# Regrouping the weight slices and the chunks of a scan-and-FFN kernel on eight cores

## The chip, the cores and the metric

The kernel runs on all 8 NeuronCores of one Trainium2 chip. Each core computes one of the 8 batch rows; nothing is exchanged between cores. The metric is the device time of the slowest core, in microseconds (us).

## The reference

The input x is 8 x 2048 x 1024 in f32. Per batch row, with D = 1024, 16 states per channel and an inner size of 4096:

```python
# part 1: a selective scan
u = layernorm(x)
delta = softplus(u @ Wd.T + bd)
a_pos = softplus(a_log) + 1e-4                      # [1024, 16]
for t in range(2048):
    state = exp(-delta[t, :, None] * a_pos) * state + delta[t, :, None] * b_param * u[t, :, None]
    y[t] = state.sum(-1)
x = x + layernorm(y @ Wo.T + bo)
# part 2: a feed-forward part with quantized weights and rows
def weight_quant(w): s = 1 / clip(mean(abs(w)), 1e-5); return clip(round(w * s), -1, 1) / s
def act_quant(v):    s = 127 / clip(max(abs(v), -1), 1e-5); return clip(round(v * s), -128, 127) / s
def bitlinear(v, w): return act_quant(v) @ weight_quant(w).T
v = layernorm(x)
x = x + layernorm(bitlinear(silu(bitlinear(v, w_gate)) * bitlinear(v, w_up), w_down))
```

w_gate and w_up are 4096 x 1024, w_down is 1024 x 4096.

## The kernel before

A row of 2048 tokens is 16 tiles of 128 tokens (NC = 16). The tiles are grouped into five chunks, CHUNK = (4, 4, 4, 2, 2), and a chunk's scan runs channel by channel and state by state over all its tokens: 128 scans (8 channel blocks x 16 states) of 512 or 256 columns for each chunk, 640 in all (NSCAN). Chunk q continues from the states that chunk q - 1 left.

Part 1 of a chunk, by engine:

- SyncE (SP) loads x tiles into two buffers; VectorE takes their statistics (`stats`, bn_stats on two halves, bn_aggr, then the negated mean and the variance plus EPS as two one-column steps); GpSimd raises the latter to the power -1/2 (`rstd`) and normalizes; TensorE transposes the tile, ScalarE copies it into `s_uT`.
- Delta: TensorE multiplies with Wd (`s_w`, shared by Wd and Wo and reloaded in turn by GpSimd's queue), ScalarE makes the softplus in four activations, GpSimd adds the two halves and then makes delta * u.
- Scan k: ScalarE makes exp(-delta * a) into one of two PSUM banks (L554), GpSimd makes delta * u * b into the ring `s_dun` (L860), VectorE runs the recurrence (L694), TensorE adds up the 16 states (L383), GpSimd copies the last column of four scans into `s_state` (L869), and ScalarE moves the sum out.
- Output: Wo on TensorE, two norms, the row quantization (`quant1`), a transpose into one of five buffers `s_q1T`.

Part 2 of a tile tc: TensorE multiplies with gate and up in two groups (`gate_up(tc, 0)` and `gate_up(tc, 1)`, each 4 banks of gate and 4 of up, 8 matmuls a bank; five PSUM banks in turn), ScalarE makes silu (L615), VectorE the product (L768) into one of three buffers `s_h` of 2048 columns, then the maximum (L772), the scale, and the quantized products (L787). `down(tc)` transposes them on TensorE (L456), ScalarE copies back (L623), and 64 matmuls with w_down follow (L472), whose quantized form comes back from HBM (`tdq`) for each tile. A tile's `down` stands on TensorE between the two groups of the next tile. The last norm is added to the output by an accumulating DMA.

The quantized weights are made inside the kernel. Each of gate, up and down is cut into 32 slices of 128 x 1024, loaded through five staging buffers `stg` (NSTG = 5). A slice is loaded twice. The first pass (P1) sums its absolute values, even slices on ScalarE (L590), odd ones on VectorE (L741); TensorE then makes the mean over partitions. The second pass (P2) scales and rounds on GpSimd (L899), and ScalarE writes the signs in FP8 (L601) into `s_tg` and `s_tu`, or into `s_tq`, from where SP stores them to `tdq`. PSEQ is the order of all 192 loads; before, it is P1 of gate, up and down, then P2 of gate and up by halves, then P2 of down. `gate_up` of tile 0 waits for 32 signed slices for its first group and 64 for its second; `loads_td` waits for all 96.

Every engine executes one order written out by hand as a string. A letter is the next step of a lane, a number repeats it. On all engines `s` is a scan step (on TensorE, four scans), `a` the first norm, `b` Delta, `c` and `d` the output and its norms; `p` is a weight slice, `g` a step of part 2 (on TensorE one bank, one transpose or 8 down matmuls; on VectorE one product, a maximum, or the scales), `t` a copied transpose, `f` the last norm, `v` a state copy, `w` a load of Wd or Wo. On SP `x` loads a tile, `p` a slice, `q` stores signs, `r` loads a down block, `o` stores the first sum.

Of the kernel before, what the change touches and what calls it, by code (L numbers as in the profile page):

```python
# [7 lines left out]
F32 = mybir.dt.float32  # L8
# [20 lines left out]
CHUNK = (4, 4, 4, 2, 2)  # L29
# [85 lines left out]
def on_act(i):  # L115
    return i % 2 == 0


P1A = [sum(on_act(j) for j in range(i)) for i in range(97)]
# [4 lines left out]
def place(k):  # L124
    q, i = k // 128, k % 128
    if LEN[q] > 256:
        return k % 3, 0, k - 2
    i += 128 * (q - min(j for j in range(NQ) if LEN[j] <= 256))
    return k % 3, 256 * (i // 3 % 2), (k - i - 2 + i % 3 if i < 6 else k - 5)


def build_nc():
# [23 lines left out]
    with ExitStack() as es:  # L156
# [18 lines left out]
        s_h = SB("s_h", [128, 3, 2048], BF16)  # L175
        s_q1T = SB("s_q1T", [128, 5, KC, 128], BF16)
# [5 lines left out]
        s_dun = SB("s_dun", [128, 3, 512], F32)  # L182
# [14 lines left out]
        s_nm = SB("s_nm", [128, 4, 2, 2], F32)  # L197
# [3 lines left out]
        s_r1u = SB("s_r1u", [128, NC], F32)  # L201
        s_r2d = SB("s_r2d", [128, NC], F32)
# [31 lines left out]

        d_cst, d_bor, d_bo2, d_o = SEM("d_cst"), SEM("d_bor"), SEM("d_bo2"), SEM("d_o")
# [20 lines left out]
        def gid(tc, grp):  # L258
            return (2 * tc + grp) % 3
# [84 lines left out]
        def _(h):  # L344
# [43 lines left out]
            def out_proj():  # L388
                for tc in range(NC):
# [5 lines left out]
                    if tc == 0:  # L395
                        h.wait_ge(d_bo2, 16)
# [583 lines left out]
```

## Time and profile before

| | |
|---|---|
| time, median of 3 runs | 1418.84 us (1415.46 to 1420.03) |
| the profiled execution: its time | 1418.27 us |
| its span on the slowest core (core 0) | 1416.7 us |
| spans of the eight cores | 1403.5 to 1416.7 us |
| TensorE, VectorE, ScalarE, GpSimd busy | 1025, 1043, 898, 771 us |
| HBM read, written | 218.38 MB, 20.97 MB |

The span runs from the first to the last instruction of the core; the device time lies 1.6 us above it. Busy times are of one core. A TensorE clock of 1.00 is full speed.

### The profile page before, as it was taken

The page shows a single profiled execution, that of the slowest core. Times are in us where ns is not written, and L with a number is a line of the kernel's source. Part 1 is how long each engine was busy: PE and PEld are TensorE (multiplying, and loading weights), DVE is VectorE, ACT ScalarE, POOL GpSimd, SP SyncE. Part 2 cuts the span into 40 slices and gives each one's busy share as a digit, 9 for nine tenths or more (in the row PEclk, how much of TensorE's full clock was granted, in tenths as well). Part 3 has the DMA queues.
Part 4 walks back from the last instruction along what each step waited for, and adds up shares of the span by engine and source line. Part 5 has one row for each costly group of instructions (what it writes and reads, how often), then busy time and mean ns, then how long its engine had stood idle before and what let it go on. Part 6 is the DMA issues. An engine that isn't in the chain of part 4 may idle for free.

```text
span 1416.7 us, 21053 instructions; the slowest of 8 cores (1403.5 to 1416.7 us)
## 1 busy us (share of the span) xinstructions
PE 1025.1 (72%) x5094; PEld 473.7 (33%) x5094; DVE 1042.7 (74%) x1390; ACT 898.1 (63%) x1348; POOL 771.1 (54%) x1116
## 2 busy tenths in 40 slices
PE   0445333231766588989899879899899989989994
PEld 0211000010322144444444434444444444444442
DVE  2468999555768898789999898888677887854221
ACT  0788777787869758855567864656775576533121
POOL 1476654899878765666445566464465643430000
PEclk9967555556878699999999999999999999999997
DMA  8996988799797683525624162474137341422442
GB/s 178 281 279 209 248 269 266 246 281 266 229 276 216 210 187 102 108 50 176 152 87 135 30 157 52 125 174 135 30 120 153 101 131 27 127 93 74 132 134 75
DMA packets 69387, 223.94 MB, mean 158 GB/s; under 512 B 7441, under 2 KB 11921, under 8 KB 69266
## 3 DMA queue, kind: packets, MB, share of 16 engines
q1 hardware_dynamic: 58642, 197.43, 44.8%
q0 software_dynamic: 10624, 25.17, 11.7%
q8 instruction: 43, 0.70, 0.2%
q14 instruction: 78, 0.64, 0.2%
HBM read 218.38 MB, written 20.97 MB: 169 GB/s over the span
## 4 chain that ended last, share of the span: by engine, by line
DVE 27%; PE 26%; issue 16%; POOL 11%; ACT 10%; DMA 8%; DVEq 1%; SPq 1%; POOLq 0%; ACTq 0%
DVE s_s L694 19%; PE p_gu L437 15%; POOL s_dun L860 8%; PE p_dn L472 5%; DMA stg<-wus 3%; ACT p_ab L554 2%; POOL stg L899 2%; DVE s_qs L772 2%; DMA stg<-wgs 1%; DMA s_onesf<-onesf 1%; PE p_y L383 1%; DMA s_td<-tdq 1%; PE p_wo L402 1%; ACT s_sg L615 1%; DVE s_h L768 1%
## 5 line engine op out<-in xcount | busy, mean ns | idle before, releaser
L554 ACT ACTIVATE p_ab<-s_dl,s_nega 128x512 f32<-128x512 bf16 (+1 forms) x640 | 380.2, 601 | 266.2 <-DVE s_s L694 264.3
L694 DVE TENSOR_TENSOR_SCAN s_s<-p_ab,s_state,s_dun 128x512 bf16<-128x512 f32 (+1 forms) x512 | 489.8, 1002 | 73.5 <-POOL s_dun L860 33.7
L860 POOL TENSOR_SCALAR s_dun<-s_uT,s_bprm 128x512 f32<-128x512 bf16 (+1 forms) x640 | 386.1, 608 | 257.1 <-DVE s_s L694 255.2
L383 PE MATMUL p_y<-s_s,s_ident 128*128 128x512 bf16 (+1 forms) x640 | 169.3, 395 | 215.5 <-DVE s_s L694 212.9
L437 PE MATMUL p_gu<-s_tu,s_q1T 128*128 128x512 fp8e4 x1024 | 240.1, 387 | 29.9 <-ACT s_sg L615 19.6
L472 PE MATMUL p_dn<-s_td,s_h 128*128 128x512 fp8e4 x1024 | 235.8, 382 | 6.1 <-ACT s_t L573 3.0
L437 PE MATMUL p_gu<-s_tg,s_q1T 128*128 128x512 fp8e4 x1024 | 231.2, 380 | 4.7 <-ACT s_tu L601 2.9
L694 DVE TENSOR_TENSOR_SCAN s_s<-p_ab,s_dun 128x512 bf16<-128x512 f32 x128 | 149.5, 1207 | 31.6 <-POOL s_dun L860 28.1
L383 PEld LDWEIGHTS p_y<-s_s,s_ident 128*128 128x128 bf16 x640 | 61.3, 105 | 318.8 <-issue 288.5
L768 DVE TENSOR_TENSOR s_h<-s_sg,p_gu 128x512 bf16<-128x512 bf16 x128 | 87.2, 683 | 98.2 <-PE p_gu L437 89.3
L437 PEld LDWEIGHTS p_gu<-s_tu,s_q1T 128*128 128x128 bf16 x1024 | 100.1, 99 | 155.4 <-issue 46.7
L819 POOL TENSOR_TENSOR s_rs<-s_nm,s_const 128x1 f32<-128x1 f32 x64 | 35.7, 557 | 204.9 <-DVE s_nm L674 204.9
L437 PEld LDWEIGHTS p_gu<-s_tg,s_q1T 128*128 128x128 bf16 x1024 | 100.1, 98 | 122.1 <-issue 6.8
L472 PEld LDWEIGHTS p_dn<-s_td,s_h 128*128 128x128 bf16 x1024 | 99.6, 99 | 121.6 <-issue 14.4
L899 POOL TENSOR_SCALAR stg<-stg,s_wsc,s_const 128x1024 f32<-128x1024 f32 x96 | 116.2, 1213 | 9.2 <-DMA stg<-wgs 3.4
L615 ACT ACTIVATE s_sg<-p_gu,s_r1g 128x512 bf16<-128x512 f32 x128 | 79.5, 687 | 34.2 <-PE p_gu L437 33.9
L623 ACT ACTIVATE s_h<-p_t 128x1024 bf16<-128x1024 int16 x64 | 61.3, 1020 | 34.3 <-PE p_t L456 34.3
L869 POOL COPY s_state<-s_s 128x4 bf16<-128x4 bf16 x128 | 24.3, 190 | 104.5 <-DVE s_s L694 103.8
L370 PE MATMUL p_b<-s_uT,s_w 128*128 128x512 bf16 (+1 forms) x320 | 67.8, 366 | 17.2 <-ACT s_uT L521 7.7
L772 DVE TENSOR_REDUCE s_qs<-s_h 128x1 f32<-128x2048 bf16 x32 | 73.1, 2285 | 3.3
L741 DVE TENSOR_REDUCE s_acc<-stg 128x1 f32<-128x1024 f32 x48 | 57.6, 1201 | 21.5 <-DMA stg<-wgs 18.8
L402 PE MATMUL p_wo<-s_w,s_dl 128*128 128x512 bf16 x256 | 65.2, 401 | 5.8 <-ACT s_t L573 3.1
(76 smaller groups left out, 1040.9 us busy)
## 6 DMA issues: line engine op xcount, KB each, us to landing
s_td<-tdq SPq DMA_DIRECT2D x128, 512.0 KB, 4.6
stg<-wgs SPq DMA_DIRECT2D x64, 512.0 KB, 6.9
stg<-wus SPq DMA_DIRECT2D x64, 512.0 KB, 6.0
stg<-wdns SPq DMA_DIRECT2D x64, 512.0 KB, 5.7
s_x<-x SPq DMA_DIRECT2D x32, 512.0 KB, 4.7
s_w<-wdT POOLq DMA_DIRECT2D x4, 2048.0 KB, 20.3
s_w<-woT POOLq DMA_DIRECT2D x4, 2048.0 KB, 19.2
out<-s_x SPq DMA_DIRECT2D x16, 512.0 KB, 4.3
```

The costliest lines, as they stand in the source:

```text
L370: i = h.matmul(p_b[ec % 2][:, 0:LEN[q]], s_w[:, kc, ec * 128:(ec + 1) * 128], s_uT[:, q % 2, kc, 0:LEN[q]], start=(kc == 0), stop=(kc == K ...
L383: i = h.matmul(p_y[:, 0:ln], s_ident[:], s_s[:, (4 * u + n) % 12, 0:ln], start=(u % 4 == 0 and n == 0), stop=(u % 4 == 3 and n == 3))
L402: h.matmul(o, s_dl[:, q % 2, kc, c * 128:(c + 1) * 128], s_w[:, kc, half * 512:(half + 1) * 512], start=(kc == 0), stop=False)
L437: i = h.matmul(bank(j % 5), s_q1T[:, tc % 5, kc, :], wt[:, 4 * grp + j % 4, kc * 512:(kc + 1) * 512], start=(kc == 0), stop=(kc == KC - 1))
L472: i = h.matmul(p_dn[:, half * 512:(half + 1) * 512], hs, s_td[:, n % 4, k4, half * 512:(half + 1) * 512], start=(kc == 0), stop=(kc == 31))
L554: h.activation(out=p_ab[:, k % 2, 0:LEN[q]], in_=s_dl[:, q % 2, dc, 0:LEN[q]], func=AF.Exp, scale=s_nega[:, k % 128:k % 128 + 1]).then_inc ...
L615: h.activation(out=s_sg[:, j, :], in_=bank(j), func=AF.Silu, scale=s_r1g[:, tc:tc + 1]).then_inc(a_si, 1)
L694: h.tensor_tensor_scan(s_s[:, k % 12, 0:LEN[q]], p_ab[:, k % 2, 0:LEN[q]], s_dun[:, b, at:at + LEN[q]], s_state[:, k % 128:k % 128 + 1] if ...
L768: h.tensor_tensor(hs[:, j * 512:(j + 1) * 512], s_sg[:, j, :], bank((4 + j) % 5), ALU.mult).then_inc(v_h, 1)
L772: step(h.tensor_reduce(qs[:, 4 + grp:5 + grp], hs, AX, ALU.max, apply_absolute_value=True))
L860: h.tensor_scalar(s_dun[:, b, at:at + LEN[q]], s_uT[:, q % 2, dc, 0:LEN[q]], s_bprm[:, k % 128:k % 128 + 1], 1.0, ALU.mult, ALU.mult).then ...
L899: h.tensor_scalar(stg[:, i % NSTG, :], stg[:, i % NSTG, :], s_wsc[:, 2 * wi + 1:2 * wi + 2], magic_ap, ALU.mult, ALU.add).then_inc(g_mg, 1)
```

## The change

It has five parts.

- CHUNK becomes (2, 4, 4, 4, 2).
- At the start SP issues the two x tiles first, then the constants, and waits for Wd before it issues the first five slices; `onesb` and `onesf` get a semaphore of their own, and the set-up steps of VectorE move behind the statistics of the second tile, with their scratch in `s_h` instead of `s_t0`.
- PSEQ becomes P1 of gate and up, P2 of gate and up by halves, P1 of down, P2 of down. The scale of the down-projection gets a lane of its own (`r` on VectorE).
- `s_h` gets four buffers, `s_q1T` four instead of five, and `down(tc - 1)` stands behind both groups of tile tc. `s_dun` is one ring of 1536 columns.
- `stats` leaves out its last two steps; GpSimd adds EPS and subtracts the mean. All five orders are written anew.

```diff
-CHUNK = (4, 4, 4, 2, 2)
+CHUNK = (2, 4, 4, 4, 2)
...
-PSEQ = [("P1", wi, j) for wi in range(3) for j in range(NSL)]
+PSEQ = [("P1", wi, j) for wi in range(2) for j in range(NSL)]
 for _h in range(2):
     PSEQ += [("P2", wi, 16 * _h + j) for wi in range(2) for j in range(16)]
+PSEQ += [("P1", 2, j) for j in range(NSL)]
 PSEQ += [("P2", 2, j) for j in range(NSL)]
...
+def places():
+    at, over, end = [], [], 0
+    for k in range(NSCAN):
+        n = LEN[k // 128]
+        o = -(-end // n) * n % 1536
+        last = [j for j in range(max(0, k - 12), k) if at[j] < o + n and o < at[j] + LEN[j // 128]]
+        at.append(o)
+        over.append(max(last) + 1 if last else 0)
+        end = o + n
+    return at, over
+DUN_AT, DUN_OVER = places()
+NH = 4
+NQT = 4
...
-            h.dma_start(out=s_bd[:], in_=d_bd).then_inc(d_cst, 16)
-            h.dma_start(out=s_bprm[:], in_=d_bprm).then_inc(d_cst, 16)
+            next(lanes["x"])
+            next(lanes["x"])
             h.dma_start(out=s_ident[:], in_=d_ident).then_inc(d_cst, 16)
             h.dma_start(out=s_nega[:], in_=d_alog).then_inc(d_cst, 16)
+            h.dma_start(out=s_bd[:], in_=d_bd).then_inc(d_cst, 16)
             h.dma_start(out=s_const[:], in_=d_const).then_inc(d_cst, 16)
-            next(lanes["x"])
-            next(lanes["x"])
-            h.dma_start(out=s_onesb[:], in_=d_onesb).then_inc(d_cst, 16)
-            h.dma_start(out=s_onesf[:], in_=d_onesf).then_inc(d_cst, 16)
-            h.dma_start(out=s_t0[0:1, 0, :], in_=d_bo).then_inc(d_bor, 16)
+            h.dma_start(out=s_bprm[:], in_=d_bprm).then_inc(d_cst, 16)
+            h.dma_start(out=s_h[0:1, 0, :].bitcast(F32), in_=d_bo).then_inc(d_bor, 16)
+            h.dma_start(out=s_onesb[:], in_=d_onesb).then_inc(d_one, 16)
+            h.dma_start(out=s_onesf[:], in_=d_onesf).then_inc(d_one, 16)
+            h.wait_ge(d_wl, 16)
             for i in range(NSTG):
                 next(lanes["p"])
...
                 for tc in range(NC):
                     yield from gate_up(tc, 0)
+                    yield from gate_up(tc, 1)
                     if tc > 0:
                         yield from down(tc - 1)
-                    yield from gate_up(tc, 1)
                 yield from down(NC - 1)
...
-                step(h.bn_aggr(s_mv[:, kd, sl, :], s_bn[:, kd, sl, :, :].rearrange("p a b -> p (a b)")))
+                h.bn_aggr(s_mv[:, kd, sl, :], s_bn[:, kd, sl, :, :].rearrange("p a b -> p (a b)")).then_inc(v_st[kd], 1)
...
-                h.tensor_scalar(s_nm[:, kd, sl, 0:1], s_mv[:, kd, sl, 0:1], -1.0, None, ALU.mult).then_inc(v_st[kd], 1)
-                h.tensor_scalar(s_nm[:, kd, sl, 1:2], s_mv[:, kd, sl, 1:2], EPS, None, ALU.add).then_inc(v_st[kd], 1)
...
-                            if j == 0 and 2 * tc + grp >= 3:
-                                h.wait_ge(t_td, 8 * ((2 * tc + grp - 3) // 2 + 1))
+                            if j == 0 and 2 * tc + grp >= NH:
+                                h.wait_ge(t_td, 8 * ((2 * tc + grp - NH) // 2 + 1))
...
+            def scale():
+                for tc in range(NC):
+                    h.wait_ge(v_q2, 2 * tc + 2)
+                    if tc == 0:
+                        h.wait_ge(v_m, 6)
+                    h.tensor_scalar(s_r2d[:, tc:tc + 1], s_q0[:, tc:tc + 1], s_wsc[:, 4:5], None,
+                                    ALU.mult).then_inc(v_r2, 1)
+                    yield
...
-                h.wait_ge(v_st[kd], 2 * tc + 2)
-                h.tensor_tensor(s_rs[:, kd, sl:sl + 1], s_nm[:, kd, sl, 1:2], negh_ap, ALU.pow).then_inc(g_own, 1)
-                cnt["own"] += 1
+                h.wait_ge(v_st[kd], tc + 1)
+                h.tensor_scalar(s_ve[:, kd, sl:sl + 1], s_mv[:, kd, sl, 1:2], EPS, None, ALU.add).then_inc(g_own, 1)
+                h.wait_ge(g_own, cnt["own"] + 1)
+                h.tensor_tensor(s_rs[:, kd, sl:sl + 1], s_ve[:, kd, sl:sl + 1], negh_ap, ALU.pow).then_inc(g_own, 1)
+                cnt["own"] += 2
```

Where the letters stand on each engine, by the number of scans ahead of them, before and after:

| | before | after |
|---|---|---|
| GpSimd: P2 slice 1, 32, 64, 96 | scan 106, 130, 154, 188 | scan 131, 181, 212, 290 |
| TensorE: first bank of gate_up(0) | scan 144 | scan 208 |
| TensorE: first down matmul of tile 0 | scan 192 | scan 296 |
| TensorE: steps of part 2 ahead of the last scan's sum, of 448 | 360 | 336 |

## Rows read from the trace of the kernel before

**Rows 1.** The page's head: the span, and busy time, share and instructions by engine.

```profile
span 1416.7 us, 21053 instructions; the slowest of 8 cores (1403.5 to 1416.7 us)
...
PE 1025.1 (72%) x5094; PEld 473.7 (33%) x5094; DVE 1042.7 (74%) x1390; ACT 898.1 (63%) x1348; POOL 771.1 (54%) x1116
```

**Rows 2.** Busy time by stretch, core 0: stretch, its length, each engine's busy us.

```profile
core 0: us, PE busy (x) PEld busy (x) DVE busy (x) ACT busy (x) POOL busy (x), PEclk, DMA share, GB/s
0.00:85.00 85.00, 28.59 (x144) 13.61 (x144) 30.01 (x56) 43.99 (x74) 27.10 (x32) 0.96 0.90 239
85.00:309.00 224.00, 71.37 (x181) 20.33 (x182) 189.46 (x174) 176.25 (x267) 156.15 (x215) 0.55 0.87 254
309.00:472.00 163.00, 88.80 (x379) 37.02 (x376) 114.50 (x144) 133.45 (x156) 140.71 (x156) 0.75 0.84 251
472.00:530.00 58.00, 46.26 (x215) 20.21 (x216) 54.30 (x64) 36.33 (x50) 37.18 (x57) 0.89 0.70 181
530.00:1240.00 710.00, 639.02 (x3389) 310.55 (x3387) 596.97 (x849) 463.51 (x751) 387.73 (x637) 0.98 0.42 109
1240.00:1404.00 164.00, 151.03 (x791) 72.03 (x789) 55.74 (x101) 43.58 (x54) 19.55 (x19) 0.98 0.37 106
```

**Rows 3.** The timeline's opening: start us, length us, what, and the idle time before.

```profile
25.55 1.28 ACT L643 ACT_TABLE_LOAD   x1 [25.55 <-DMA s_onesf<-onesf]
...
28.79 0.69 DVE L668 BATCH_NORM_STATS2 s_bn<-s_x 128x6 f32<-128x512 f32 x1
...
48.24 7.03 PE L370 MATMUL p_b<-s_uT,s_w 128*128 128x512 bf16 x24 [2.92 <-ACT s_uT L521]
...
85.03 2.34 DVE L694 TENSOR_TENSOR_SCAN s_s<-p_ab,s_dun 128x512 bf16<-128x512 f32 x2 [2.23 <-POOL s_dun L860]
```

**Rows 4.** DMA issues of Wd, in the first 60 us and in all: us to landing last.

```profile
s_w<-wdT POOLq DMA_DIRECT2D x1, 2048.0 KB, 24.9
...
s_w<-wdT POOLq DMA_DIRECT2D x4, 2048.0 KB, 20.3
```

**Rows 5.** Instructions by line: min/median/max ns, first and last start in us.

```profile
L694 DVE TENSOR_TENSOR_SCAN s_s<-p_ab,s_dun x128: 1193/1209/1225, 85.0 to 306.7; 128x512 bf16<-128x512 f32 x128
...
L899 POOL TENSOR_SCALAR stg<-stg,s_wsc,s_const x96: 1187/1194/2139, 252.8 to 474.1; 128x1024 f32<-128x1024 f32 x96
...
L437 PE MATMUL p_gu<-s_tg,s_q1T x64: 376/379/631, 362.6 to 394.3; 128*128 128x512 fp8e4 x64
```

**Rows 6.** Groups by line and shape, core 0: busy us, mean ns, idle before and releasers.

```profile
L860 POOL TENSOR_SCALAR s_dun<-s_uT,s_bprm 128x512 f32<-128x512 bf16 x384 | 264.7, 693 | 152.2 <-DVE s_s L694 151.0 <-ACT s_t L542 0.4 <-POOL s_uT L848 0.4
L554 ACT ACTIVATE p_ab<-s_dl,s_nega 128x512 f32<-128x512 bf16 x384 | 261.0, 686 | 156.1 <-DVE s_s L694 154.8
...
L694 DVE TENSOR_TENSOR_SCAN s_s<-p_ab,s_state,s_dun 128x256 bf16<-128x256 f32 x256 | 179.6, 739 | 25.9 <-ACT p_ab L554 12.7 <-POOL s_dun L860 3.5 <-POOL s_state L869 0.6
...
L554 ACT ACTIVATE p_ab<-s_dl,s_nega 128x256 f32<-128x256 bf16 x256 | 119.2, 475 | 110.2 <-DVE s_s L694 109.6
L899 POOL TENSOR_SCALAR stg<-stg,s_wsc,s_const 128x1024 f32<-128x1024 f32 x96 | 116.2, 1213 | 9.2 <-DMA stg<-wgs 3.4 <-DMA stg<-wus 3.3 <-DMA stg<-wdns 2.0
...
L741 DVE TENSOR_REDUCE s_acc<-stg 128x1 f32<-128x1024 f32 x48 | 57.6, 1201 | 21.5 <-DMA stg<-wgs 18.8 <-DMA stg<-wus 2.7
L590 ACT ACTIVATE stg<-stg 128x1024 f32<-128x1024 f32 x48 | 50.0, 1043 | 4.4 <-DMA stg<-wgs 4.4
...
L601 ACT ACTIVATE s_tu<-stg,s_const 128x1024 fp8e4<-128x1024 f32 x32 | 36.1, 1141 | 7.5 <-POOL stg L899 6.4
...
L819 POOL TENSOR_TENSOR s_rs<-s_nm,s_const 128x1 f32<-128x1 f32 x64 | 35.7, 557 | 204.9 <-DVE s_nm L674 204.9
...
L590 ACT ACTIVATION_READ_ACCUMULATOR stg<-stg 128x1 f32 x48 | 9.0, 187 | 0.0
```

**Rows 7.** Near the end: one piece of the chain, and one row of the timeline.

```profile
1322.45 27.63 PE p_gu L437 x128
...
1386.58 3.38 PE L456 MATMUL p_t<-s_ident,s_h 128*128 128x128 bf16 x32 [6.51 <-DVE s_h L787]
```

More of the change, by code:

```diff
@@ L107, with on_act @@
 W_OF["C", NQ - 1] = W_OF["C", NQ - 2]
-PSEQ = [("P1", wi, j) for wi in range(3) for j in range(NSL)]
+PSEQ = [("P1", wi, j) for wi in range(2) for j in range(NSL)]
 for _h in range(2):
     PSEQ += [("P2", wi, 16 * _h + j) for wi in range(2) for j in range(16)]
+PSEQ += [("P1", 2, j) for j in range(NSL)]
 PSEQ += [("P2", 2, j) for j in range(NSL)]
[L115 to L129, printed above, removed]
+def on_act(wi, j):
+    return j % 2 == 0
+N1A = [sum(e[0] == "P1" and on_act(*e[1:]) for e in PSEQ[:i]) for i in range(len(PSEQ) + 1)]
+N1V = [sum(e[0] == "P1" and not on_act(*e[1:]) for e in PSEQ[:i]) for i in range(len(PSEQ) + 1)]
+N2 = [sum(e[0] == "P2" for e in PSEQ[:i]) for i in range(len(PSEQ) + 1)]
+def places():
[11 more added lines that the diff above has]
+NQT = 4
 def build_nc():
@@ L436, in gate_up @@
                     for kc in range(KC):
-                        i = h.matmul(bank(j % 5), s_q1T[:, tc % 5, kc, :],
+                        i = h.matmul(bank(j % 5), s_q1T[:, tc % NQT, kc, :],
                                      wt[:, 4 * grp + j % 4, kc * 512:(kc + 1) * 512],
@@ L736, in weights @@
             def weights():
-                for i in range(96):
-                    wi = i // NSL
-                    if not on_act(i):
+                for i, (what, wi, j) in enumerate(PSEQ):
+                    if what == "P2":
+                        continue
+                    if not on_act(wi, j):
                         h.wait_ge(d_stg[i % NSTG], 16 * (i // NSTG + 1))
-                        h.tensor_reduce(s_acc[:, i:i + 1], stg[:, i % NSTG, :], AX, ALU.add,
+                        h.tensor_reduce(s_acc[:, 32 * wi + j:32 * wi + j + 1], stg[:, i % NSTG, :], AX, ALU.add,
                                         apply_absolute_value=True).then_inc(v_p1, 1)
                         yield
-                    if i % NSL == NSL - 1:
-                        h.wait_ge(a_p1, P1A[i + 1])
-                        h.wait_ge(v_p1, i + 1 - P1A[i + 1])
+                    if j == NSL - 1:
+                        h.wait_ge(a_p1, N1A[i + 1])
+                        h.wait_ge(v_p1, N1V[i + 1])
                         h.tensor_reduce(s_asum[:, wi:wi + 1], s_acc[:, 32 * wi:32 * (wi + 1)], AX,
@@ L876, in second_ln @@
                     i = X_OF["C", tc]
[L877 to L878 removed]
+                    mean, rs = rstd(1, tc)
+                    h.tensor_scalar(t0, t0, mean, rs, ALU.subtract, ALU.mult).then_inc(g_st[1], 1)
                     h.wait_ge(g_st[1], tc + 1)
@@ L886, in third_ln @@
                     q = QOF[tc]
-                    nm, rs = rstd(2, tc)
+                    mean, rs = rstd(2, tc)
                     h.wait_ge(g_x1, tc + 1)
-                    h.tensor_scalar(s_t0[:, T0_OF["C", q, tc - FIRST[q]] % 2, :], s_x[:, X_OF["C", tc] % 2, :], nm, rs,
-                                    ALU.add, ALU.mult).then_inc(g_st[2], 1)
+                    h.tensor_scalar(s_t0[:, T0_OF["C", q, tc - FIRST[q]] % 2, :], s_x[:, X_OF["C", tc] % 2, :], mean, rs,
+                                    ALU.subtract, ALU.mult).then_inc(g_st[2], 1)
                     yield
             def weights():
-                for i in range(96, 192):
-                    wi = PSEQ[i][1]
+                for i, (what, wi, j) in enumerate(PSEQ):
+                    if what == "P1":
+                        continue
                     h.wait_ge(d_stg[i % NSTG], 16 * (i // NSTG + 1))
-                    if i == 96:
-                        h.wait_ge(v_m, 6)
+                    if j == 0:
+                        h.wait_ge(v_m, 2 * wi + 2)
                     h.tensor_scalar(stg[:, i % NSTG, :], stg[:, i % NSTG, :], s_wsc[:, 2 * wi + 1:2 * wi + 2],
```

171 lines of the change are left out of this document (86 added, 85 removed).

## The prediction

> **What bounds the kernel now.** I read the page first for the sums. The span is 1416.7 us; TensorE is busy 1025 us of it and VectorE 1043 us, so neither is full on average and the average says nothing yet [rows 1]. So I cut the span into stages at the points where the work changes, and asked for busy time per engine in each [rows 2]. Five regimes show.
>
> To 85 us nothing is scanned. The first Delta matmul starts at 48.24 us and the first scan at 85.03 us; ScalarE does nothing until 25.55 us, when the last constant lands, and the first statistics come at 28.79 us [rows 3]. From 85 to 309 us the 128 scans of the first chunk run [rows 5], with VectorE busy 189.5 of 224 us. From 309 to 472 us GpSimd is the fullest engine (140.7 of 163 us) and ScalarE is close behind (133.5): each slice's second pass goes through these two. GpSimd's rounding of slices runs from 252.8 to 474.1 us [rows 5]. The feed-forward part (FFN) can't start before its first slices are done: its first matmul is at 362.6 us [rows 5]. From 530 to 1240 us TensorE is busy 639 of 710 us, and from 1240 to 1404 us 151 of 164 us: here TensorE sets the pace, with VectorE second (597 of 710) [rows 2]. So the end is decided by two numbers: the time X at which all slices are through and TensorE can run without holes, and the TensorE work left at X. The chip's clock does not disturb this: it is granted at 0.98 of full speed after 530 us, and it is half speed (1.2 of 2.4 GHz) mostly where TensorE has little to do, 0.55 from 85 to 309 us [rows 2].
>
> **The start.** The change issues two x tiles first and Wd beside them, then the constants, and holds the first five slices until Wd has landed. In the kernel before, Wd took 24.9 us from issue, against a median of 20.3 us over its four loads [rows 4]. With the slices held back I take 20.3, so it lands near 22 us. The first chunk now needs two normalized tiles, not four, and x tiles 2 and 3, which stood behind slices, no longer hold it. The five constants now stand behind 1 MB of x; unless they land after 22 us nothing waits for them, and the set-up steps of VectorE that stood ahead of the first statistics are moved behind the second tile. From the first Delta matmul to the first scan there were 36.8 us [rows 3], mostly ScalarE's. The columns halve, and the same engine's exponential goes from 686 to 475 ns [rows 6], a ratio of 0.69: 25 us at most, 23 with fewer slices in between. First scan: 22 + 1 + 23 = 46 us, 39 us earlier. Bounds: 42 us, and 60 us if constants or tile copies come late.
>
> **The first chunk.** Counting the written orders between scan 0 and scan 128: VectorE has 128 scans at 0.70 us, 28 slice sums at 1.20 and some 4 us of small work, 127 us; ScalarE has 128 exponentials at 0.47 (60), six narrow and eight wide Delta blocks of four activations each at 0.47 and 0.69 (33), 32 slice sums at 1.04 plus the 0.19 to read the sum (39), and 7 of copies, 139 us [rows 6]. VectorE's span over busy was 224/189.5 = 1.18 before [rows 2], which would give 150. Between 139 and 150 I take 146, as ScalarE leads in the first half and VectorE in the second. Scan 128 ends at 192 us, against 309. It is not a free gain of 117 us: it holds half the columns, and 32 slices fewer.
>
> **The slices.** PSEQ now runs both passes of gate and up and then both of down, so 192 slices as before. Counting the orders from scan 128 to scan 288, just before which the last slice is written on GpSimd (its 96th at scan 290): GpSimd has 93 roundings at 1.21 us (112), 160 products at 0.69 (110), and 56 us of states, deltas and norms, 279 us; ScalarE has 160 exponentials at 0.69 (109), 108 slice steps (125) and 59 of others, 293 us; VectorE 272 us [rows 6]. Taken in pieces of 32 scans, the fullest engine changes (VectorE 44, GpSimd 60, ScalarE 67, VectorE 75, GpSimd 58): 305 us. The stage 309 to 472 us ran at 163/140.7 = 1.16 times its fullest engine [rows 2]; made from the same counts in pieces of 32 scans it is 149 us, a ratio of 1.09. 305 x 1.09 = 333; 293 x 1.16 = 340. I take 334, with 319 (293 x 1.09) as the low end. The high end is the ratio over scans 128 to 224, 221 us for 181 of counted work, 1.22: 357. So X, at scan 288, is 192 + 334 = 526 us.
>
> **What is left at X.** This is where the change gives back. In the kernel before at 530 us (scan 224) the orders leave TensorE 780 us at full clock, by counts and row durations; the rows show 639 + 151 = 790 busy in 874 us, so 84 us of holes [rows 2]. The new order at scan 288 leaves 798 us, because tile 0's down-projection waits for the down slices and stands at scan 296: only two tiles' gate and up are done by then. So 790 + 18 = 808 busy. The holes: one goes for certain, the 6.51 us for which TensorE waits for the last tile's quantized products [rows 7]; now both halves of gate and up of tile 15 are followed by tile 14's down, 17 us of cover. VectorE has 27 us less to do in this stretch by counts (671 to 644): 352 scans stand there instead of 416, and one-column steps are removed. I credit half, 14 us. 808 + 84 - 6.5 - 14 = 871 us. Ends: 848 (half of the holes) and 892 (holes grow with the two engines both nearer full). The end of TensorE's work: 526 + 871 = 1397, against 1404.
>
> **Edits costed at nothing.** The negated mean goes: one VectorE step less per norm, and the EPS step moves from VectorE to GpSimd. No row shows it there; below it is 0, above it is the 0.56 us of the power on one column. I take 0.25, 64 times, 16 us of GpSimd, which is busy 388 of 710 us after 530 us; 11 of the 64 lie in the slices' stage and are in its 279. The scale of the down-projection becomes a step of its own (16 x 0.2 us), covered by VectorE's idle share. Four product buffers and four, not five, q1T buffers: a tile's q1T now waits for gate and up of the tile four earlier, which the order has done. The ring for B u holds the same 1536 columns. If that cover fails, these cost about 10 us together.
>
> **A rule against the change.** A long run of gate and up shows 128 matmuls of 512 columns in 27.63 us, 216 ns each, in a program on all eight cores [rows 7]. The Trainium skill, page "TensorE: Matmul & The Clock Gate", Part 1, states a peak-current limit of 13/16 of the clock once three cores of a die run dense matmuls; by it the same matmul would take 266 ns, and a denser order would gain nothing. By that rule the 808 us would be about 990, and the end some 180 us later. The row disagrees with it, so I give it under 1 in 50, inside the slower case.
>
> **The sum.** 46 + 146 + 334 + 871 = 1397 us; after TensorE's last matmul there are 12.8 us to the span's end [rows 1, 2] and 1.6 us around it (1418.27 against 1416.7). That is 1411 against 1418.27, less 0.5%; the profiled run is 0.6 us below the median of 1418.84, so nothing is corrected. I say **1410 us**.
>
> **The rivals.** *Back to even*: the holes don't shrink as I credit, and half of their growth in ratio (808 x 874/790 = 894, less 6.5 is 888) comes: 526 + 880 + 14 = 1420. For it: the two engines' loads from scan 320 to 512 are nearly equal. *Slower, by the slices*: with ScalarE, GpSimd and VectorE loaded to 293, 279 and 272 us in one stage, each waits for both others, and the ratio is 1.22: X is 549, end 549 + 871 + 14 = 1434, and 1440 with the extra small waits. It decides against the change from X = 533 on (1404 - 871). *Clearly faster*: TensorE, with weights whole and two tiles in hand, runs at 95% instead of 90%: 808/0.95 = 851, less some at the start (first scan at 42): 1375 to 1385. Against it: VectorE already sits at 84% there. *The change doesn't do what it says*: the first scan isn't earlier, as constants come late; then 1425.
>
> **Chances.** Forecast, 1392 to 1414: 0.38. Clearly faster, under 1392: 0.18. Even, 1415 to 1423: 0.19. Slower (slices, growing holes, late start): 0.25. A measurement of this kernel can tell about 0.3% from no change. Faster 0.56, same 0.19, slower 0.25. The range takes most of both outer cases: 1382 to 1438; the forecast's own is 1392 to 1425.
>
> **What will show it.** The first scan near 46 us, scan 128 done near 192, the last slice rounded near 526 us, TensorE's holes from there to the end below 80 us, and no wait of its transposes at the end. Wrong if the slices' stage passes 345 us, or if products wait for scans so that TensorE has over 90 us of holes.

## The result, and the profile after

The changed kernel takes 1500.9 us (median of 6 runs) against 1416.8 us for the kernel before on the same chip: a ratio of 1.059 (95% interval 1.058 to 1.061), slower by 5.9%. The prediction said 1410 us, 0.6% faster, with a range to 1438 us: wrong in sign and in size. A first measurement gave 1520.4 us and a ratio of 1.067 (1.049 to 1.085); in most of its executions one die ran at a lower clock, so the rows below are those of the second.

The head of the page of the changed kernel, core 6:

```profile
span 1498.8 us, 21022 instructions; the slowest of 8 cores (1485.1 to 1498.8 us)
## 1 busy us (share of the span) xinstructions
PE 1047.4 (70%) x5094; PEld 479.6 (32%) x5094; DVE 1015.7 (68%) x1262; ACT 892.3 (60%) x1344; POOL 953.8 (64%) x1180
```

Against [rows 1] one number stands out. GpSimd (POOL) is busy 954 us instead of 771, while VectorE and ScalarE have lost a little. The 64 new EPS steps can't be it: the groups by line and shape give them 15.8 us in all.

```profile
L920 POOL TENSOR_SCALAR s_t<-s_x,s_mv,s_rs 128x1024 f32<-128x1024 f32 x16 | 60.6, 3790 | 4.2 <-POOL s_rs L851 3.0 <-DVE s_s L724 1.3
L948 POOL TENSOR_SCALAR s_f<-s_f,s_mv,s_rs 128x1024 f32<-128x1024 f32 x16 | 60.6, 3789 | 3.3 <-POOL s_rs L851 3.3
L861 POOL TENSOR_SCALAR s_t<-s_x,s_mv,s_rs 128x1024 bf16<-128x1024 f32 x16 | 60.6, 3788 | 5.9 <-POOL s_rs L851 3.4 <-PE p_lnT L374 2.5
L909 POOL TENSOR_SCALAR s_t<-s_t,s_mv,s_rs 128x1024 f32<-128x1024 f32 x16 | 60.6, 3788 | 3.0 <-POOL s_rs L851 3.0
L849 POOL TENSOR_SCALAR s_ve<-s_mv 128x1 f32<-128x1 f32 x64 | 15.8, 247 | 189.6 <-DVE s_mv L688 171.3 <-DMA s_bprm<-bprm 15.7
```

The four wide norm steps take 3.79 us each. In the kernel before, one of them is the second-last GpSimd row of the timeline's end:

```profile
1408.02 1.19 POOL L916 TENSOR_SCALAR s_f<-s_f,s_nm,s_rs 128x1024 f32<-128x1024 f32 x1 [0.18 <-POOL s_rs L819]
```

Same tile, same shape; the diff changes `ALU.add` with the negated mean into `ALU.subtract` with the mean. 64 steps x 2.60 us are 166 us, and with the 16 us of EPS steps that is all of GpSimd's rise.

Where the time went by stage: the same table as [rows 2], cut at the first scan, scan 128, the last rounded slice and the last scan.

```profile
0.00:58.00 58.00, 15.04 (x96) 10.52 (x96) 14.09 (x21) 22.93 (x51) 26.41 (x27) 0.89 0.78 192
58.00:198.00 140.00, 49.10 (x210) 22.39 (x210) 114.38 (x166) 110.91 (x226) 101.07 (x194) 0.59 0.82 235
198.00:582.00 384.00, 172.41 (x662) 66.11 (x662) 268.50 (x281) 284.09 (x372) 309.99 (x349) 0.69 0.71 208
582.00:1295.00 713.00, 630.05 (x3161) 294.32 (x3162) 555.25 (x694) 425.47 (x638) 465.58 (x578) 0.96 0.39 108
1295.00:1483.00 188.00, 180.59 (x967) 86.22 (x965) 61.96 (x100) 47.80 (x59) 45.21 (x30) 1.00 0.39 118
```

In the slices' stage GpSimd is now the fullest engine (310 of 384 us, ScalarE 284), and the stage takes 384 us, over the 345 that the prediction named as a sign of being wrong. In the stage of the steady work (582 to 1295 us) no engine is full: TensorE 88%, VectorE 78%, GpSimd 65%. The time must go into waits of one engine for another.

### The profile page after: what moved, and what is told of

It is laid out like the page before. It is cut to its first block, busy times and chain, and to the rows that moved or that the text cites. A ratio compares the mean times of both kernels' runs of the same rounds, so it can differ in the third digit from the quotient of the medians.

```text
span 1524.4 us, 20970 instructions; the slowest of 8 cores (1490.2 to 1524.4 us)
## 1 busy us (share of the span) xinstructions
PE 1078.0 (71%) x5042; PEld 490.9 (32%) x5094; DVE 1017.0 (67%) x1262; ACT 892.9 (59%) x1344; POOL 954.1 (63%) x1180
## 4 chain that ended last, share of the span: by engine, by line
PE 26%; POOL 22%; DVE 18%; issue 17%; DMA 8%; ACT 7%; DVEq 1%; POOLq 0%; SPq 0%; ACTq 0%
PE p_gu L456 13%; DVE s_s L724 12%; POOL s_dun L891 7%; PE p_dn L491 7%; POOL stg L931 3%; POOL s_t L909 3%; ACT p_ab L570 2%; POOL s_f L948 2%; POOL s_t L861 2%; DMA s_td<-tdq 2%; PE p_wo L420 2%; DMA s_w<-woT 2%; POOL s_t L920 2%; PE p_y L400 1%; PE p_b L387 1%
## 5 line engine op out<-in xcount | busy, mean ns | idle before, releaser
L724 DVE TENSOR_TENSOR_SCAN s_s<-p_ab,s_state,s_dun 128x512 bf16<-128x512 f32 (+1 forms) x512 | 558.8, 1135 | 116.5 <-POOL s_dun L891 79.4
L400 PE MATMUL p_y<-s_s,s_ident 128*128 128x512 bf16 (+1 forms) x605 | 164.9, 404 | 265.8 <-DVE s_s L724 263.5
L456 PE MATMUL p_gu<-s_tu,s_q1T 128*128 128x512 fp8e4 x1024 | 253.4, 405 | 16.5 <-ACT s_sg L631 13.3
L491 PE MATMUL p_dn<-s_td,s_h 128*128 128x512 fp8e4 x1024 | 249.1, 402 | 10.9 <-DMA s_td<-tdq 7.5
L456 PE MATMUL p_gu<-s_tg,s_q1T 128*128 128x512 fp8e4 x1024 | 246.3, 398 | 7.1 <-ACT s_q1T L597 5.5
L456 PEld LDWEIGHTS p_gu<-s_tu,s_q1T 128*128 128x128 bf16 x1024 | 104.2, 103 | 154.8 <-issue 69.5
L849 POOL TENSOR_SCALAR s_ve<-s_mv 128x1 f32<-128x1 f32 x64 | 15.8, 247 | 216.2 <-DVE s_mv L688 197.1
L724 DVE TENSOR_TENSOR_SCAN s_s<-p_ab,s_dun 128x256 bf16<-128x256 f32 x128 | 81.5, 677 | 26.5 <-ACT p_ab L570 16.1
L420 PE MATMUL p_wo<-s_w,s_dl 128*128 128x512 bf16 x246 | 69.6, 431 | 7.4 <-DMA s_w<-woT 4.8
L651 ACT ACTIVATE s_f<-p_dn,s_r2d 128x1024 f32<-128x1024 f32 x16 | 17.8, 1110 | 89.7 <-PE p_dn L491 89.7
```

Source lines behind the costliest of these rows:

```text
L400: i = h.matmul(p_y[:, 0:ln], s_ident[:], s_s[:, (4 * u + n) % 12, 0:ln], start=(u % 4 == 0 and n == 0), stop=(u % 4 == 3 and n == 3))
L420: h.matmul(o, s_dl[:, q % 2, kc, c * 128:(c + 1) * 128], s_w[:, kc, half * 512:(half + 1) * 512], start=(kc == 0), stop=False)
L456: i = h.matmul(bank(j % 5), s_q1T[:, tc % NQT, kc, :], wt[:, 4 * grp + j % 4, kc * 512:(kc + 1) * 512], start=(kc == 0), stop=(kc == KC - 1))
L491: i = h.matmul(p_dn[:, half * 512:(half + 1) * 512], hs, s_td[:, n % 4, k4, half * 512:(half + 1) * 512], start=(kc == 0), stop=(kc == 31))
L724: h.tensor_tensor_scan(s_s[:, k % 12, 0:LEN[q]], p_ab[:, k % 2, 0:LEN[q]], s_dun[:, DUN_AT[k]:DUN_AT[k] + LEN[q]], s_state[:, k % 128:k % ...
```

## The experiments

The theory after the profile: GpSimd's wide step is slow because of its operation, and this alone turned a small gain into the loss. The rival: the new order of chunks and slices is what costs, and the slow step is mostly hidden.

**Norm steps as before (e1), and the same operation in the kernel before (e2).** e1 is the changed kernel with the `stats` and `rstd` of the kernel before and `ALU.add`; e2 is the kernel before with one operand and one operation changed.

```diff
# e2, in the kernel before, for all four norms; e1 is the reverse in the changed kernel, with both one-column steps back on VectorE
-                return s_nm[:, kd, sl, 0:1], s_rs[:, kd, sl:sl + 1]
+                return s_mv[:, kd, sl, 0:1], s_rs[:, kd, sl:sl + 1]
...
-                                    ALU.add, ALU.mult).then_inc(g_st[0], 1)
+                                    ALU.subtract, ALU.mult).then_inc(g_st[0], 1)
```

> The changed kernel with the norm steps of the kernel before: VectorE makes the negated mean and the variance plus EPS, GpSimd adds and multiplies. If GpSimd's slower norm step (3.79 us in the changed kernel against 1.19 us, 64 times, 166 us) is the cause, GpSimd's busy time falls from 954 to about 770 us, the last slice is rounded near 526 us instead of 581 us, and the time is 1395 to 1425 us. If the new order of slices and chunks is the cause, the step falls to 1.19 us all the same, but the time stays above 1460 us, with the last slice still after 560 us.

> The kernel before with one thing changed: GpSimd subtracts the mean where it added the negated mean (VectorE still makes both columns). If the operation is what costs, the norm step takes 3.8 us here too, GpSimd's busy time rises from 771 to about 937 us, and the time rises by 40 to 110 us, since the kernel before has the same chains. If the cause lies in the new order, the operation costs nothing here: below 1425 us.

Measured: e1 1397.4 us, ratio 0.988 (0.985 to 0.991); e2 1488.8 us, ratio 1.051 (1.049 to 1.053). So the changed kernel with the old norm steps is faster than the kernel before by 1.2%, and the kernel before with the subtraction alone is slower by 5.1%, or 73 us; its GpSimd is busy 937.7 us, where 937 was expected. The rival falls. The head of e1's page, and one group by line and shape of e2:

```profile
span 1394.2 us, 21086 instructions; the slowest of 8 cores (1385.3 to 1394.2 us)
...
PE 1023.2 (73%) x5094; PEld 473.2 (34%) x5094; DVE 1031.3 (74%) x1390; ACT 892.6 (64%) x1344; POOL 766.9 (55%) x1116
```

```profile
L889 POOL TENSOR_SCALAR s_t<-s_x,s_mv,s_rs 128x1024 f32<-128x1024 f32 x16 | 60.5, 3780 | 3.9 <-POOL s_rs L819 3.6 <-DVE s_s L694 0.2
```

GpSimd is back at 767 us in e1. One expectation missed: the last slice was to be rounded near 526 us and was at 542 (below).

**The negation on GpSimd (e3).** Is it the operation, or the operand's place and the extra steps?

```diff
                 h.tensor_scalar(s_ve[:, kd, sl:sl + 1], s_mv[:, kd, sl, 1:2], EPS, None, ALU.add).then_inc(g_own, 1)
+                h.tensor_scalar(s_ng[:, kd, sl:sl + 1], s_mv[:, kd, sl, 0:1], -1.0, None, ALU.mult).then_inc(g_own, 1)
...
-                return s_mv[:, kd, sl, 0:1], s_rs[:, kd, sl:sl + 1]
+                return s_ng[:, kd, sl:sl + 1], s_rs[:, kd, sl:sl + 1]
...
-                                    ALU.subtract, ALU.mult).then_inc(g_st[0], 1)
+                                    ALU.add, ALU.mult).then_inc(g_st[0], 1)
```

> The changed kernel with its EPS step on GpSimd kept, and one more one-column step there that negates the mean, so that the wide step adds. If subtract alone makes the wide step slow, it is 1.19 us here and the time is that of the first kernel of this call within 10 us, though GpSimd has two one-column steps of 0.25 us more for each norm (32 us). If the place of the operand or GpSimd's extra steps and waits matter, it stays more than 20 us above it.

Measured: 1399.5 us, ratio 0.990 (0.986 to 0.994), 2 us from e1. The groups show the cheap way to the same norm: 0.22 us for the negation, 1.20 for the wide step.

```profile
L923 POOL TENSOR_SCALAR s_t<-s_x,s_ng,s_rs 128x1024 f32<-128x1024 f32 x16 | 19.1, 1196 | 4.3 <-POOL s_rs L854 4.3
...
L851 POOL TENSOR_SCALAR s_ng<-s_mv 128x1 f32<-128x1 f32 x64 | 14.2, 222 | 5.3
```

**The operations by themselves (e8).** e1 with single steps behind the last one; its time of 1433.9 us includes them.

```diff
+            for op0, op1 in ((ALU.add, ALU.mult), (ALU.subtract, ALU.mult), (ALU.mult, ALU.subtract),
+                             (ALU.mult, ALU.add), (ALU.subtract, ALU.add), (ALU.max, ALU.mult)):
+                for w in (512, 1024):
+                    h.wait_ge(g_own, cnt["own"])
+                    h.tensor_scalar(b[:, 0:w], a[:, 0:w], c0, c1, op0, op1).then_inc(g_own, 1)
+                    cnt["own"] += 1
```

> The same base, with single steps behind the last one: GpSimd's two-operation step on 128 x 512 and 128 x 1024 f32 with add and mult, subtract and mult, mult and subtract, mult and add, subtract and add, max and mult, then a plain add and a plain subtract of two tiles, and the first three pairs on VectorE. If subtract as such is slow on GpSimd, every pair with it takes 3.8 us at 1024 columns and the plain subtract is slower than the plain add; if only one pair is, the others take 1.2 us. On VectorE all are alike. Slow by the column: 512 columns take half.

The timeline, in the order of the code above, two widths for each pair; the last row is a plain add and a plain subtract of two tiles:

```profile
1392.70 0.76 POOL L976 TENSOR_SCALAR s_t<-s_t,s_mv,s_rs 128x512 f32<-128x512 f32 x1 [4.59 <-DMA out<-s_f]
1393.63 1.20 POOL L976 TENSOR_SCALAR s_t<-s_t,s_mv,s_rs 128x1024 f32<-128x1024 f32 x1 [0.17 <-POOL s_t L976]
1395.00 2.09 POOL L976 TENSOR_SCALAR s_t<-s_t,s_mv,s_rs 128x512 f32<-128x512 f32 x1 [0.17 <-POOL s_t L976]
1397.26 3.78 POOL L976 TENSOR_SCALAR s_t<-s_t,s_mv,s_rs 128x1024 f32<-128x1024 f32 x1 [0.17 <-POOL s_t L976]
...
1403.47 3.78 POOL L976 TENSOR_SCALAR s_t<-s_t,s_mv,s_rs 128x1024 f32<-128x1024 f32 x1 [0.17 <-POOL s_t L976]
...
1408.37 1.20 POOL L976 TENSOR_SCALAR s_t<-s_t,s_mv,s_rs 128x1024 f32<-128x1024 f32 x1 [0.17 <-POOL s_t L976]
...
1412.01 3.78 POOL L976 TENSOR_SCALAR s_t<-s_t,s_mv,s_rs 128x1024 f32<-128x1024 f32 x1 [0.17 <-POOL s_t L976]
...
1418.21 3.78 POOL L976 TENSOR_SCALAR s_t<-s_t,s_mv,s_rs 128x1024 f32<-128x1024 f32 x1 [0.17 <-POOL s_t L976]
1422.14 4.82 POOL L980 TENSOR_TENSOR s_x<-s_t,s_x 128x1024 f32<-128x1024 f32 x2
```

At 1024 columns add and mult take 1.20 us, and so do mult and add; every other pair tried takes 3.78: subtract and mult, mult and subtract, subtract and add, but also max and mult. The plain steps on two tiles are alike for add and subtract (2.34 us each of the 4.82). So "subtract is slow" was too narrow: of the two-operation steps on GpSimd, the two orders of add and mult are short, and every pair with subtract or max that was tried is 3.15 times as long at 1024 columns. Most of it is a cost by the column: 512 more columns add 0.44 us to the short steps and 1.69 us to the long ones. Why the long ones are long, no run shows. On VectorE the three pairs tried take 0.55 us at 512 columns and 0.81 at 1024, whatever the operation.

The Trainium skill, page "GPSIMD Engine Reference", section 3.1, gives 769 ns for 512 elements as GpSimd's best case, and says nothing of a pair's operations. The 0.76 us of the short pair at 512 columns agrees. By the same cost per element 1024 columns would take 1.54 us, an estimate from the page's figure; measured are 1.20, so its figure doesn't carry over to that width.

**Which norm costs (e4, e5, e6, e10).** Each is e1 with the subtraction put back in some norms: the last (e4), the first (e5), the second and third (e6), all four (e10). The negated mean and EPS stay on VectorE.

```diff
# e4; the others are the same edit in their norm
                     mean, rs = rstd(3, tc)
-                    h.tensor_scalar(s_f[:], s_f[:], mean, rs, ALU.add, ALU.mult).then_inc(g_st[3], 1)
+                    mean = s_mv[:, 3, tc % 2, 0:1]
+                    h.tensor_scalar(s_f[:], s_f[:], mean, rs, ALU.subtract, ALU.mult).then_inc(g_st[3], 1)
```

> The first kernel of this call, but the last norm alone (16 of 64, behind the down-projection) subtracts. If the cost is GpSimd's load in the whole, a quarter of the loss comes back, some 20 us. If it is the norms that stand ahead of TensorE's work (first, second and third), this one costs only its length at the very end, 2.6 us, up to 6 us.

> The changed kernel with the norm steps of the kernel before, but the first norm (16 of 64) subtracts on GpSimd. The last norm alone cost 12 us, all four about 105. If the loss follows GpSimd's load wherever it stands, this is 12 to 26 us. If a slow norm costs only where it holds up the scans or TensorE, most of this one is early: two before the first scan (some 5 us of delay) and four in the first chunk, where GpSimd is free; then 8 to 15 us in all.

> The same base, but the second and third norm (32 of 64) subtract on GpSimd. They stand one behind the other between the output projection and the quantized rows that the gate and up matmuls need, with five of sixteen tiles inside the stage in which GpSimd rounds the slices. If the chain matters, this is the largest part of the loss, 50 to 75 us; if the load alone does, twice the last norm's, 24 to 50 us.

> The same base with all four norms subtracting on GpSimd and nothing else, the negated mean and EPS still on VectorE. The three parts alone cost 16 (first norm), 50 (second and third) and 12 us (last), 78 together. If they add up, this is 1475 us; if each late norm also takes the slack that hid the others, it is 1490 to 1510 us, as the changed kernel, and then the EPS step on GpSimd has no part in the loss.

| kernel | norms that subtract | time, us | over e1 | ratio to before |
|---|---|---|---|---|
| e1 | none | 1397.4 | | 0.988 (0.985 to 0.991) |
| e4 | last, 16 | 1409.3 | 12 | 0.995 (0.993 to 0.998) |
| e5 | first, 16 | 1413.6 | 16 | 0.998 (0.997 to 1.000) |
| e6 | second and third, 32 | 1447.5 | 50 | 1.021 (1.018 to 1.023) |
| e10 | all, 64 | 1486.2 | 89 | 1.048 (1.046 to 1.051) |
| changed kernel (e11) | all, and EPS on GpSimd | 1500.9 | 104 | 1.059 (1.058 to 1.061) |

Per slow step: 0.74 us for the last norm, 1.0 for the first, 1.57 for the two between, of the 2.6 us that each is longer. e4's 12 us lie between what its two theories gave (20, or up to 6): no other engine waits for the last norm's output, but its steps stand in GpSimd's fixed order between products for scans. e6's 50 us lie at the low edge of what the chain theory gave and at the high edge of the load theory, so its time doesn't tell them apart. The parts add up to 78 us, all four cost 89: a little more than the sum. In the kernel before the same four cost 73 (e2), so the new order is the more sensitive one.

The traces do tell them apart. In e6 VectorE waits for the outputs of the second and third norm (the same two waits in e1: 18.7 and 9.6 us):

```profile
DVE s_bn L685 <- POOL s_x L914: 55.3, 15, 7.4
...
DVE s_r L752 <- POOL s_t L923: 34.6, 11, 6.0
```

The waits that GpSimd's steps end, for each kernel, in us on its slowest core; e9, the next experiment, adds load alone:

| kernel | time over e1 | VectorE for the second and third norm (s_x, s_t) | TensorE for the first norm (p_lnT) | scans for products (s_dun) |
|---|---|---|---|---|
| e1 | | 28 | 30 | 60 |
| e4, last | 12 | 32 | 31 | 70 |
| e5, first | 16 | 28 | 48 | 60 |
| e6, second and third | 50 | 90 | 33 | 63 |
| e9, load alone | 31 | 36 | 37 | 84 |
| e10, all | 89 | 91 | 52 | 83 |

A longer norm lengthens the wait for that norm's output (e5, e6), and load that nobody waits for lengthens the scans' wait for products (e4, e9). e10 has both.

**Load or length (e9).** e1 with added work on GpSimd, meant to match what the subtraction adds, but behind each norm's hand-over, where nobody waits for it.

```diff
+            def load():
+                for n in range(11):
+                    h.tensor_scalar(s_junk[:, n:n + 1], negm_ap, 1.0, None, ALU.add)
...
                     ALU.add, ALU.mult).then_inc(g_st[0], 1)
+                    load()
```

> The changed kernel with the norm steps of the kernel before (1397 us), and behind each of the 64 wide steps of a norm, after what it hands on, eleven one-column steps on GpSimd that nobody waits for, about 2.6 us, so that GpSimd is as loaded as with the subtraction while the norm itself is not longer. If GpSimd's load is what costs (products for the scans and rounded slices come late), most of the loss of about 100 us is here: 1460 us or more. If the norm's own length on the way to TensorE is what costs, the time stays below 1430 us.

Measured: 1428.7 us, ratio 1.008 (1.005 to 1.011), 31 us over e1. The eleven steps are shorter than planned; the head of the page has GpSimd at

```profile
PE 1026.3 (72%) x5094; PEld 472.7 (33%) x5094; DVE 1033.5 (72%) x1390; ACT 893.9 (63%) x1344; POOL 890.0 (62%) x1820
```

so 123 us of load against the subtraction's 168 (935.4 in e10 less 766.9). In proportion, 168 us of load would cost 43 us. It was to be under 1430 or over 1460, and is just under: both ways count. About half of the 89 us comes from GpSimd being busy when products are wanted, the other half from the norm itself being longer. That split is an estimate, as it scales e9's loss. The scans' waits for products fit it: they grow by 23 us in e9 and by 22 in e10, where the rest of the growth is in the waits for norms.

**The start (e7).** e1 with SP's start of the kernel before: constants, then x, and slices not held back.

```diff
-            next(lanes["x"])
-            next(lanes["x"])
             h.dma_start(out=s_ident[:], in_=d_ident).then_inc(d_cst, 16)
...
             h.dma_start(out=s_const[:], in_=d_const).then_inc(d_cst, 16)
+            next(lanes["x"])
+            next(lanes["x"])
...
-            h.wait_ge(d_wl, 16)
```

> The same base (no subtraction), with the start of the kernel before on SP: constants first, then x, and the slices not held back for Wd. If the earlier start is what the remaining gain of 1.2% rests on, the first scan comes 10 to 20 us later than 47 us and the time rises by as much, to 1407 to 1417 us. If the slices' stage takes it up anyway, the time stays within 4 us of 1397 us.

Measured: 1395.6 us, ratio 0.986 (0.983 to 0.988), as e1. The timelines say why. e7 first, then e1:

```profile
11.95 1.28 ACT L659 ACT_TABLE_LOAD   x1 [11.95 <-DMA s_const<-constv]
...
15.94 0.69 DVE L684 BATCH_NORM_STATS2 s_bn<-s_x 128x6 f32<-128x512 f32 x1 [13.68 <-DMA s_x<-x]
...
26.25 5.69 PE L386 MATMUL p_b<-s_uT,s_w 128*128 128x256 bf16 x32 [1.80 <-DMA s_w<-wdT]
```

```profile
5.14 0.69 DVE L685 BATCH_NORM_STATS2 s_bn<-s_x 128x6 f32<-128x512 f32 x1 [2.87 <-DMA s_x<-x]
...
17.53 1.28 ACT L660 ACT_TABLE_LOAD   x1 [17.53 <-DMA s_bprm<-bprm]
...
25.20 6.29 PE L387 MATMUL p_b<-s_uT,s_w 128*128 128x256 bf16 x32 [1.37 <-ACT s_uT L540]
```

With x first, the statistics start 11 us earlier, but the constants land behind x, and ScalarE and GpSimd wait for them until 17.5 us; Wd lands 4.4 us sooner (20.1 against 24.5 us from issue). The first Delta matmul is 1 us earlier. The first scan is at 47.2 us in e1 and at 48.3 in e7, so the order of the loads is worth 1 us there and nothing in the time. What moved the first scan from 85 to 48 us is in the edits that e7 keeps: the first chunk needs two tiles and half the columns, VectorE's set-up no longer stands ahead of the statistics, and `onesb` and `onesf` have their own semaphore. The last two show in the rows: ScalarE's first step waits in the kernel before for `onesf` until 25.55 us, and the statistics come behind it at 28.79 [rows 3]; in e7, with SP's old order, they start at 11.95 and 15.94. What each of the three is worth was not tried apart.

**The changed kernel once more (e11).** No edit.

> The changed kernel itself once more, with more rounds, since its first measurement held only one run whose dies were alike (1502 us). With all four norms subtracting and the EPS step on VectorE it is 1486 us. If the EPS step on GpSimd costs on top, this stays 10 us or more above it; if it costs nothing, as it did without the subtraction (1399.5 against 1397.4 us), this is 1482 to 1492 us.

Measured: 1500.9 us, 15 us over e10. So moving the one-column steps from VectorE to GpSimd, where 64 EPS steps of 0.25 us are new, costs 15 us beside the slow steps, though in e3, without slow steps, twice as many one-column steps on GpSimd cost 2 us.

## Why the prediction was wrong

The step that failed is under "Edits costed at nothing". It named the negated mean that goes and the EPS step that moves, priced the latter, and passed over the third edit of the same lines: the wide step's operation. The step's 1.19 us stayed in the counts as in the kernel before, though no row there shows a subtraction on GpSimd, and none of the rivals prices it. With a step on two tiles as an upper bound (the plain add takes 2.39 us on average there) it would have been up to 64 x 1.20 = 77 us more of load, and still too little. Measured: 3.79 us, 166 us more of load, and with the EPS steps 104 us of time (1500.9 against e1's 1397.4).

With that edit undone, the sum can be checked term by term. The windows of e1, core 1:

```profile
0.00:47.00 47.00, 15.31 (x96) 10.55 (x96) 15.73 (x29) 22.77 (x51) 15.30 (x23) 0.90 0.85 219
47.00:181.00 134.00, 50.21 (x208) 22.59 (x209) 114.25 (x169) 110.25 (x226) 94.17 (x191) 0.58 0.87 250
181.00:544.00 363.00, 171.71 (x666) 65.32 (x663) 272.61 (x308) 285.22 (x374) 275.69 (x339) 0.69 0.75 221
544.00:1191.00 647.00, 604.92 (x3162) 288.62 (x3163) 562.90 (x766) 425.21 (x637) 356.82 (x541) 0.99 0.44 120
1191.00:1382.00 191.00, 181.02 (x966) 86.11 (x964) 64.06 (x116) 48.29 (x60) 22.25 (x22) 1.00 0.40 116
```

| term, us | predicted | e1 | changed |
|---|---|---|---|
| to the first scan | 46 | 47 | 58 |
| to scan 128 | 146 | 134 | 140 |
| slices' stage | 334 | 363 | 384 |
| from there to TensorE's end | 871 | 838 | 901 |
| span's end, and around it | 14 | 15 | 18 |
| time | 1410 | 1397 | 1501 |

Without the failed step the sum would have been 13 us off, inside the forecast of 1392 to 1414, and that is in part luck: its terms are off by +1, -12, +29 and -33 us, which nearly cancel.

- **The start.** 46 us was right for e1, and its reason half wrong: the loads' order was given a part, and e7 shows that it has next to none. In e5, where the first norm alone is slow, the first scan is at 56.1 us instead of 47.2; so most of the way to the changed kernel's 58 is that norm, of which four steps stand ahead of the first scan.
- **The first chunk.** 12 us too high, and not by the waits: VectorE's span over busy is 134/114.25 = 1.17, near the 1.18 taken over. The counts were too high. VectorE was counted at 127 us and is busy 114, ScalarE at 139 and is busy 110. The six narrow Delta blocks counted here (11 us) and four of the 32 slice sums (5 us) are done before the first scan. For the rest, means times counts give more than the busy time: 128 scans were counted as 128 x 0.70 = 90 us, and their mean is 0.68 here, but as the records of neighbouring steps overlap they fill only 81.5.
- **The slices' stage.** 29 us too low in e1. ScalarE is busy 285 of 363 us, a ratio of 1.27 where I took 1.14 and set 1.22 as the high end. The loads themselves were counted well: 273, 285 and 276 us for VectorE, ScalarE and GpSimd, against 272, 293 and 279. With three engines so loaded each waits for the others: this is the mechanism of the rival "Slower, by the slices", which put X at 549 us; e1 has 544. Both of the prediction's signs against the change, a stage over 345 us and X past 533, are there in e1, and it is faster all the same, because of the next term.
- **What is left at X.** 808 us of TensorE work were forecast after X, and e1 has 605 + 181 = 786, with 52 us of holes instead of 63. That tile 0's down-projection comes after X was right. Some 10 of the 22 us are the granted clock, 0.99 and 1.00 where the kernel before has 0.98 (an estimate, 1 to 2% of 786); the rest was not followed up. The gain of the change is here: the kernel before had 84 us of holes [rows 2]. Its single wait of 6.5 us before the last tile's transposes [rows 7] is gone in e1. Which of the edits (four buffers, both groups in one go, the order) shrank the others was not tried.
- **Edits costed at nothing.** For the EPS step alone the price was right (e3: 2 us with two such steps), and it was wrong beside slow steps (15 us). Holding the loads back costs nothing and gives nothing (e7). The buffers were not tried by themselves.
- **The rivals.** The loss didn't come by any of them. In the changed kernel TensorE has 901 - 811 = 90 us of holes after X. Its own busy time there is 25 us above e1's for the same matmuls, and the granted clock between 582 and 1295 us is 0.96, where e1 has 0.99: 605 x 0.99/0.96 = 624 of the 630 us, an estimate. The lower clock comes together with more holes (713 - 630 = 83 us against 647 - 605 = 42 us); that the holes bring it is not shown by a run of its own.

The waits show the path of the slow step. In the changed kernel:

```profile
DVE s_bn L685 <- POOL s_x L912: 64.5, 15, 7.8
...
PE p_lnT L374 <- POOL s_t L861: 56.9, 9, 23.5
...
DVE s_r L749 <- POOL s_t L920: 40.8, 11, 6.8
```

and in e1:

```profile
PE p_lnT L374 <- POOL s_t L862: 29.5, 7, 19.8
...
DVE s_bn L685 <- POOL s_x L913: 18.7, 10, 4.8
...
DVE s_r L752 <- POOL s_t L921: 9.6, 5, 2.5
```

VectorE waits 77 us more for the outputs of the second and third norm, in order, with its scans behind them; 62 of them are there in e6 already, where only these two norms subtract. That is why the two middle norms cost most per step. VectorE is at 68% in the changed kernel, and GpSimd at 64%: the share of busy time told nothing of this.

The fastest versions are e7 and e1, 1395.6 and 1397.4 us, which lie no further apart than runs of one kernel do; both are faster than the kernel before (0.986 and 0.988).

## What to carry to other kernels

Read the diff for operations, not only for instructions: a step of the same shape on the same engine with another operation is a step that the trace doesn't show, and it needs a price or a probe of its own. When an engine is lightly used on average, a longer step there still costs, here 0.7 to 1.6 us for each 2.6 us, because every engine's order is fixed and others wait behind it. A sum that is checked term by term shows errors that cancel in the total. And if several engines reach nearly the same load in one stage, take the stage longer than the fullest of them by more than a stage with one full engine showed.

## What the runs showed of the hardware

GpSimd's two-operation step on 128 x 1024 f32 takes 1.20 us for add and mult or mult and add, and 3.78 us for subtract and mult, mult and subtract, subtract and add, and max and mult; on VectorE three of the same pairs take 0.81 us alike. The plain add and subtract of two tiles on GpSimd take 2.34 us both.

The rival of a lower clock under dense matmuls, which the prediction gave under 1 in 50, shows in the first profile of the changed kernel (core 0), but not in its second, from which the rows above are. First profile, then second:

```profile
1200.00:1250.00 50.00, 49.73 (x218) 22.75 (x217) 34.87 (x53) 26.81 (x45) 26.81 (x42) 0.81 0.32 93
...
1218.99 8.58 PE L456 MATMUL p_gu<-s_tu,s_q1T 128*128 128x512 fp8e4 x32
```

```profile
1200.00:1250.00 50.00, 44.18 (x243) 21.84 (x241) 35.73 (x56) 27.48 (x47) 28.97 (x42) 1.00 0.33 98
...
1222.52 5.34 PE L456 MATMUL p_gu<-s_tu,s_q1T 128*128 128x512 fp8e4 x24 [0.59 <-ACT s_sg L631]
```

The granted clock is 0.81 of full speed (2.4 GHz) in the one and 1.00 in the other, and a matmul of 512 columns takes 268 and 223 ns. The Trainium skill, page "TensorE: Matmul & The Clock Gate", Part 1, states a level of 13/16 of the clock as a limit on peak current; the 0.81 agrees with it, and the 1.00, with all eight cores at work, does not. The level does occur, but it is no part of the 5.9%: the execution of the second profile takes 1500.4 us.
